# Projection stage of an attention and convolution kernel: row maxima through two pairs of PSUM banks, queries and keys with one bank each

## The chip, the cores and the metric

One NeuronCore of a Trainium2 chip runs the whole program. Its engines are TensorE (PE), VectorE (DVE), ScalarE (ACT), GpSimd (POOL) and SyncE (SP), which issues most of the transfers. They run apart from each other and meet at semaphores. The metric is the device time of one execution in microseconds.

## The reference

The input is x, 2 x 256 x 64 x 64 in f32. Layer 0 is a group norm (32 groups), an attention with 4 heads of 64 channels over the 4096 positions, an output projection and a residual. Layer 1 is batch norm, relu, a 3x3 convolution with one-bit weights, once more the same, and a residual. The part that the change touches, for one batch element:

```python
xn  = group_norm(x, gn_weight, gn_bias)
qkv = einsum('oc,bchw->bohw', qkv_weight, xn) + qkv_bias      # projection
q, k, v = split(qkv, 3, axis=1)                               # 4 heads of 64 channels
attn = softmax(einsum('bhdk,bhdq->bhkq', q, k) / sqrt(64))
out  = einsum('bhkq,bhdq->bhdk', attn, v)
```

## The kernel before, in words

The attention runs over four pairs of heads (two batch elements, two pairs each); a pair fills the 128 partitions. Each pair has a projection stage and then eight query blocks of 512 queries (`query_block`). PSUM has eight banks of 128 x 512 f32. In the query blocks banks 0 to 3 hold the scores (`ps_s`, two slots of two banks), 4 and 5 the products whose maximum is sought (`ps_max`), 6 the output (`ps_o`), and 7 the half sums and the denominators (`ps_misc`).

The projection stage goes over eight blocks `kb` of 512 positions (`kb = n2 * 2 + s`, `s` is 0 or 1). For each block TensorE makes Q (index `j` = 0) and K (`j` = 1), L635, each of two products over the two halves `c` of the channels, and V, L650, of eight small products. These are f32, and each of them stands in the trace as two MATMUL rows, so Q or K is x4 and V is x16. ScalarE copies Q and K to `y32` (L545) and rounds them to f16 as `q_hi` and `k_hi` (L549), and copies V to `vals` (L552). GpSimd makes the rests `q_lo` (L470) and `k_lo` (L477) and normalizes the input two blocks ahead (`xn`, L490), once V of the block that used the same buffer is done. SP loads x for it (L425).

The softmax subtracts a row maximum, which has to be known before the first scores. So the stage also computes maxima. A unit is the product of 128 queries of a block with 512 keys, for two heads: two f16 matmuls (L662) into one pair of banks, and one reduction by VectorE from there (L803). For the first query block there are 32 units: beside block kb (kb = 1 to 7) its four units with the keys of block kb - 1 (`units_beside`), for kb = 4 to 7 one more ("early", it belongs to the second query block), and after block 7 the last four (`last_first_maxima`). `PLACE` numbers the units in the order in which they are issued. The order is written out by hand and is the same on both engines. Below, M0 to M3 are the four units beside a block, E the early one, and L0 to L3 the last four.

All units but L1 and L2 go through `ps_max`. `maxima_of` on TensorE waits until VectorE has reduced all units before (`mx_used`, which starts at 1), and VectorE waits for `mx_ready`. In a block the order is: first product of Q, E, second product of Q, M0, K, M1, half of V, M2, half of V, M3. After L3 VectorE takes the maximum over the blocks (L817), negates it (L820), and TensorE transposes it (`max_rows`, L686) for the scores (L714, L719).

Q and K of block kb go to slot s of `ps_s`, so they have two banks each in turn, and V goes to bank 6 for s = 0 and to bank 7 for s = 1 (`ps_v`). The other users of these banks are waited for: bank 6 is read by the copy of the last pair's output (`o_copied`), bank 7 holds the denominators of the last pair's last query block until VectorE has divided by them (`norm_done`; column sums L694, reciprocal L836, multiplication L845), and `ps_s` holds the output projection at the end of the first batch element (L754), which VectorE reads in `residual` (L899, `x1_ready`).

Of the kernel before, what the change touches and what calls it, by code (L numbers as in the profile page):

```python
# [19 lines left out]
ALU = mybir.AluOpType  # L20
ACT = mybir.ActivationFunctionType
F32 = mybir.dt.float32
F16 = mybir.dt.float16
AX = mybir.AxisListType
RMAX = bass.bass_isa.ReduceOp.max

P = 128
# [339 lines left out]
def attention(nc, x, qkv_t, w0_t, x1_d, g):  # L367
# [4 lines left out]
    with ExitStack() as ctx:  # L372
# [13 lines left out]
        m_part = sb("m_part", [P, 2, 2, UNITS])  # L386
        m_max = sb("m_max", [P, 2 * QT])
        m_neg = sb("m_neg", [P, 2 * QT])
        ps_v = [g.ps_o, g.ps_misc]
        acc_dve = g.ps_misc  # L390

        xn_ready = sem("xn_ready")
# [144 lines left out]
        def _(act):  # L537
            def project(b, hp, n2, s):

                pn = (b * 2 + hp) * NB + n2 * 2 + s  # L540
                for j in range(2):
                    act.wait_ge(g.proj_ready, 4 + pn * 3 + j + 1)

                    act.wait_ge(klo_done if j else qlo_done, 1 + pn)
                    nc.scalar.activation(y32[:, s, j], g.ps_s[:, s, j], ACT.Identity,  # L545
                                         bias=g.qk_bias[:, hp + 2 * j:hp + 2 * j + 1],
                                         scale=g.fscale[:, j:j + 1]).then_inc(y_ready, 1)
                    act.wait_ge(y_ready, 4 + pn * 2 + (j + 1))
                    nc.scalar.activation((k_hi if j else q_hi)[:, cols(n2 * 2 + s)], y32[:, s, j],  # L549
                                         ACT.Copy).then_inc(hi_ready, 1)  # L550
                act.wait_ge(g.proj_ready, 4 + (pn + 1) * 3)
                nc.scalar.activation(vals[:, (n2 * 2 + s) * QT:(n2 * 2 + s + 1) * QT, :],  # L552
                                     ps_v[s].rearrange("p (t d) -> p t d", t=QT), ACT.Copy).then_inc(v_copied, 1)

            def softmax(it, first, last):

# [59 lines left out]
        def _(pe):  # L616
            mm = nc.tensor.matmul

            def project(b, hp, n2, s):

                it0 = (b * 2 + hp) * NB
                pn = it0 + n2 * 2 + s
                pe.wait_ge(g.w_staged, 16 * (b * 2 + hp + 1))
                pe.wait_ge(xn_ready, (pn + 1) * CB)

                pe.wait_ge(y_ready, 2 + pn * 2)
                if n2 == 0:
                    pe.wait_ge(x1_ready, (b * NB + 1 + s) * CB)
                kb = n2 * 2 + s
                these, early = units_beside(kb) if kb else ([], [])  # L630
                if kb > 1:
                    pe.wait_ge(hi_ready, 2 * (it0 + kb - 1))
                for j in range(2):
                    for c in range(CB):
                        ins = mm(g.ps_s[:, s, j], wst[:, c, j, :], xn[:, s, c, :], start=(c == 0), stop=(c == CB - 1))  # L635
                        if c == CB - 1:
                            ins.then_inc(g.proj_ready, 1)
                        if j == 0 and c == 0:
                            maxima_of(it0, early)
                        if kb and c:  # L640
                            if j == 0:
                                pe.wait_ge(hi_ready, 2 * (it0 + kb))
                            maxima_of(it0, these[j:j + 1])
                pe.wait_ge(v_copied, 1 + pn)
                if n2 == 0:

                    pe.wait_ge(norm_done if s else o_copied, it0 * NP + NP if s else it0 + 1)
                for t in range(QT):
                    for c in range(CB):
                        last = mm(ps_v[s][:, t * P:(t + 1) * P], xn[:, s, c, t * P:(t + 1) * P], wst[:, c, 2, :],  # L650
                                  start=(c == 0), stop=(c == CB - 1))
                    if t == 1:
                        maxima_of(it0, these[2:3])
                last.then_inc(g.proj_ready, 1)
                maxima_of(it0, these[3:4])

            def maximum(it0, unit, into):

                block, u = unit
                t, kb = u // NB, u % NB  # L660
                for h in range(2):
                    last = mm(into[:, h], q_hi[own[h], block * TB + t * P:block * TB + (t + 1) * P],  # L662
                              k_hi[own[h], kb * TB:(kb + 1) * TB], start=True, stop=True)
                last.then_inc(mx_ready, 1)

            def maxima_of(it0, units):

                for unit in units:
                    pe.wait_ge(mx_used, 1 + it0 * UNITS + PLACE[unit])
                    maximum(it0, unit, g.ps_max)  # L670

            def last_first_maxima(it0):

                units = units_beside(NB)[0]
                pe.wait_ge(hi_ready, 2 * (it0 + NB))
                pe.wait_ge(mx_used, 1 + it0 * UNITS + PLACE[units[0]])
                maximum(it0, units[0], g.ps_max)
                maximum(it0, units[1], g.ps_s[:, 0])
                maximum(it0, units[2], g.ps_s[:, 1])
                pe.wait_ge(mx_used, 1 + it0 * UNITS + PLACE[units[1]])  # L680
                maximum(it0, units[3], g.ps_max)

            def max_rows(it):
                pe.wait_ge(m_neg_ready, it + 1)
# [102 lines left out]
        def _(dve):  # L787
# [7 lines left out]
            for s in range(2):  # L795
                dve.sem_inc(g.y_out[s], 16)

            def maxima_of(it0, units, where=()):

                for i, unit in enumerate(units):  # L800
                    block, u = unit
                    dve.wait_ge(mx_ready, it0 * UNITS + PLACE[unit] + 1)
                    v.tensor_reduce(m_part[:, block % 2, :, u], where[i] if where else g.ps_max, AX.X,  # L803
                                    ALU.max).then_inc(mx_used, 1)

            def project_step(it0, kb):

                these, early = units_beside(kb)
                maxima_of(it0, early)
                maxima_of(it0, these)  # L810

            def negate_max(it):

# [98 lines left out]
            for b in range(B):  # L912
                for hp in range(2):
                    it0 = (b * 2 + hp) * NB
                    if hp:
                        for part in range(NP):
                            divide(it0 - 1, part)
                    for kb in range(1, NB):
                        project_step(it0, kb)
                    maxima_of(it0, units_beside(NB)[0], (g.ps_max, g.ps_s[:, 0], g.ps_s[:, 1], g.ps_max))  # L920
                    negate_max(it0)
                    write_max_rows(it0, 0)
                    for qb in range(NB):
                        query_block(it0 + qb, qb)
                for n2 in range(NB // 2):
                    if n2 == 1:
                        for part in range(NP):
                            divide((b + 1) * 2 * NB - 1, part)
                    for s in range(2):
                        residual(b, n2, s)  # L930
                        statistics(b, n2, s)
# [370 lines left out]
```

## Time and profile before

| what | us |
|---|---|
| median of 3 runs | 2934.8 (2934.6 to 2935.26) |
| the profiled execution, its time | 2934.27 |
| its span, from the first to the last instruction | 2932.5 |
| mean granted TensorE clock in it | 0.988 |
| TensorE matmul busy | 2793.7 (95%) |
| VectorE busy | 2117.5 (72%) |
| GpSimd busy | 2027.3 (69%) |
| ScalarE busy | 1402.7 (48%) |

Busy is the time in which an engine had an instruction in work; the duration of one is counted from its start to its modelled end. Matmuls overlap: the next starts before the one before has ended, so costs are read from start to start. A bracket behind a row of the timeline gives the idle time of the engine before it and what ended it.

### The profile page before, as it was taken

To read this page: it belongs to the slowest core of one execution; us is meant where nothing else is said; L and a number is where in the kernel's file an instruction comes from. 1 tells how busy PE (TensorE), PEld (TensorE's weight loads), DVE (VectorE), ACT (ScalarE), POOL (GpSimd) and SP (SyncE) were. 2 spreads that over 40 slices of the span, in tenths; PEclk is the share of its full clock that TensorE was granted. 3 is DMA by queue.
4 is the path that set the end of the run, shared out by engine and by line. 5 is a ranking of instruction groups with operands and counts; after the bars stand their busy time and mean duration, and the time that the engine had idled before them with its cause. 6 is when DMAs were issued, how large, how long until landed. Compare 5 with 4: busy or idle time off the path is not lost. (4 is left out here: it accounts for less than half of the span.)

```text
span 2932.5 us, 43630 instructions
## 1 busy us (share of the span) xinstructions
PE 2793.7 (95%) x17060; PEld 1013.2 (35%) x17060; DVE 2117.5 (72%) x2496; ACT 1402.7 (48%) x1477; POOL 2027.3 (69%) x1208
## 2 busy tenths in 40 slices
PE   5899999998999999998999999989999999799898
PEld 3333333333333333343333333343333333244343
DVE  5688888726777888456788888267777885588785
ACT  3355555553555555533555555534555555254342
POOL 2588888893888888844888888947888888500022
PEclk9999999999999999999999999999999999999999
DMA  5000000001000000041000000010000000421022
GB/s 213 35 1 1 1 1 1 1 5 60 1 1 1 1 1 1 1 153 42 1 1 1 1 1 1 1 44 1 1 1 1 1 1 1 148 79 60 15 100 86
DMA packets 26820, 78.27 MB, mean 27 GB/s; under 512 B 1921, under 2 KB 2177, under 8 KB 25601
## 3 DMA queue, kind: packets, MB, share of 16 engines
q1 hardware_dynamic: 25792, 74.19, 7.3%
q8 instruction: 125, 2.05, 0.3%
q10 hardware_dynamic: 832, 1.45, 0.1%
q14 instruction: 71, 0.57, 0.1%
HBM read 58.86 MB, written 16.78 MB: 26 GB/s over the span
## 5 line engine op out<-in xcount | busy, mean ns | idle before, releaser
L512 POOL TENSOR_TENSOR acc_pool<-acc_pool,prob 128x512 f32<-128x512 f32 (+1 forms) x992 | 1781.0, 1795 | 297.5 <-ACT prob L567 177.0
L803 DVE TENSOR_REDUCE m_part<-ps 128x2 f32<-128x1024 f32 x1024 | 1250.6, 1222 | 479.8 <-PE ps L662 456.0
L567 ACT ACTIVATE prob<-ps,exp_scale 128x1024 f32<-128x1024 f32 x1024 | 1086.9, 1111 | 1015.7 <-PE ps L719 1007.8
L703 PE MATMUL ps<-prob,vals 128*64 128x512 f32 x4096 | 990.9, 605 | 0.0
L662 PE MATMUL ps<-k_hi,q_hi 64*128 64x512 f16 x2048 | 394.3, 383 | 45.3 <-DVE m_part L803 45.3
L703 PEld LDWEIGHTS ps<-prob,vals 128*64 128x64 f32 x4096 | 248.7, 136 | 501.9 <-issue 364.2
L714 PE MATMUL ps<-q_hi,k_hi 64*128 64x512 f16 x2048 | 391.1, 379 | 0.0
L714 PE MATMUL ps<-q_hi,k_lo 64*128 64x512 f16 x2048 | 390.4, 378 | 0.0
L719 PE MATMUL ps<-m_rows,shift 64*128 64x512 f16 x2048 | 389.9, 377 | 0.4
L714 PE MATMUL ps<-q_lo,k_hi 64*128 64x512 f16 x2048 | 390.2, 378 | 0.0
L869 DVE TENSOR_TENSOR ps<-ps,prob 128x512 f32<-128x512 f32 x480 | 331.5, 691 | 72.4 <-ACT prob L567 72.4
L662 PEld LDWEIGHTS ps<-k_hi,q_hi 64*128 64x128 f16 x2048 | 99.3, 93 | 529.3 <-DVE m_part L803 405.2
L1135 PE MATMUL ps<-parts,signs 128*128 128x512 f16 x768 | 181.3, 385 | 21.9 <-DVE parts L1194 19.8
L836 DVE RECIPROCAL ps<-ps 128x128 f32<-128x128 f32 x128 | 122.7, 958 | 84.4 <-PE ps L694 84.4
L1135 PE MATMUL ps<-parts,wmid 128*128 128x512 f16 x768 | 178.8, 383 | 0.0
L719 PEld LDWEIGHTS ps<-m_rows,shift 64*128 64x128 f16 x2048 | 99.9, 94 | 125.4 <-DVE m_rows L827 4.0
L714 PEld LDWEIGHTS ps<-q_lo,k_hi 64*128 64x128 f16 x2048 | 100.1, 94 | 122.6 <-issue 2.2
L714 PEld LDWEIGHTS ps<-q_hi,k_hi 64*128 64x128 f16 x2048 | 100.3, 95 | 117.1 <-ACT prob L567 45.4
L714 PEld LDWEIGHTS ps<-q_hi,k_lo 64*128 64x128 f16 x2048 | 100.0, 94 | 113.3 <-issue 1.1
L635 PE MATMUL ps<-xn,wst 128*128 128x512 f32 x256 | 131.3, 628 | 5.0 <-ACT xn L595 4.7
L1085 ACT ACTIVATE parts<-comb 128x512 f16<-128x512 f32 x128 | 77.4, 632 | 105.7 <-DVE comb L1215 105.7
L1135 PEld LDWEIGHTS ps<-parts,signs 128*128 128x128 f16 x768 | 75.2, 98 | 115.9 <-DVE parts L1194 19.9
(109 smaller groups left out, 1408.3 us busy)
## 6 DMA issues: line engine op xcount, KB each, us to landing
xt<-in_x SPq DMA_DIRECT2D x40, 512.0 KB, 4.3
xf<-in_x SPq DMA_DIRECT2D x4, 2048.0 KB, 16.5
x_scratch<-y_tile SPq DMA_DIRECT2D x16, 512.0 KB, 5.0
wf<-in_w_t SPq DMA_DIRECT2D x4, 1152.0 KB, 8.9
rows<-x_scratch SPq DMA_DIRECT2D x8, 576.0 KB, 5.3
rows<-x_scratch SPq DMA_DIRECT2D x8, 544.0 KB, 4.6
xn<-in_x SPq DMA_DIRECT2D x8, 512.0 KB, 5.6
xt<-x_scratch SPq DMA_DIRECT2D x4, 1024.0 KB, 5.1
```

What stands on the lines that cost most here:

```text
L512: nc.gpsimd.tensor_tensor(acc[:, part], acc[:, part], tile[:, part], ALU.add).then_inc(pool_add, 1)
L567: nc.scalar.activation(prob[:, n % PBUF], g.ps_s[:, kt % 2].rearrange("p h n -> p (h n)"), ACT.Exp, scale=g.exp_scale[:]).then_inc(exp_don ...
L635: ins = mm(g.ps_s[:, s, j], wst[:, c, j, :], xn[:, s, c, :], start=(c == 0), stop=(c == CB - 1))
L662: last = mm(into[:, h], q_hi[own[h], block * TB + t * P:block * TB + (t + 1) * P], k_hi[own[h], kb * TB:(kb + 1) * TB], start=True, stop=True)
L703: last = mm(g.ps_o[own[h], :], vals[:, kt, own[h]], prob[:, n % PBUF, h * TB:(h + 1) * TB], start=(kt == 0), stop=(kt == KT - 1))
L714: mm(g.ps_s[:, kt % 2, h], k[own[h], keys], q[own[h], cols(qb)], start=(k is k_hi and q is q_hi), stop=False)
L719: last = mm(g.ps_s[:, kt % 2, h], shift[own[h]], m_rows[own[h], qb % 2], start=False, stop=True)
L803: v.tensor_reduce(m_part[:, block % 2, :, u], where[i] if where else g.ps_max, AX.X, ALU.max).then_inc(mx_used, 1)
L836: v.reciprocal(g.ps_misc[:, c], g.ps_misc[:, c]).then_inc(rec_ready, 1)
L869: v.tensor_tensor(acc_dve, acc_dve, tile, ALU.add).then_inc(dve_add, 1)
L1085: nc.scalar.activation(parts[:, k % 2, c, 0, pos, :, 1:W + 1], comb[:, c, pos], ACT.Copy).then_inc(hi_done, 1)
L1135: last = nc.tensor.matmul(g.ps[:, 4 * m + pos, :], weights(l, c, pos, dx)[:, m * P:(m + 1) * P], parts[:, s, c, h, pos, :, dx:dx + W], sta ...
```

## The change

The pairs of banks in the projection stage are laid out anew. The maxima go in turn through banks 4, 5 and banks 6, 7 (`max_pair`, by the parity of `PLACE`), and TensorE waits only until the unit before the last one is reduced. Q has bank 0 and K bank 1 for every block, V has bank 2 for s = 0 and bank 3 for s = 1. The units are issued in twos: Q, E if there is one, K, M0 and M1, all of V, M2 and M3. The waits for other users of the banks move with them: `o_copied` and `norm_done` before the first unit of block 1, `x1_ready` for the second slot of the output projection before V of block 0. Q and K each wait until ScalarE has read that of the block before (`y_ready`). The last four units: L0 and L1 through the two pairs, L2 through banks 0 and 1, L3 through the pair of L1. VectorE's order of units is as before, and nothing is added to or taken from the work.

```diff
--- before.py
+++ after.py
@@ -386,7 +386,7 @@
         m_part = sb("m_part", [P, 2, 2, UNITS])
         m_max = sb("m_max", [P, 2 * QT])
         m_neg = sb("m_neg", [P, 2 * QT])
-        ps_v = [g.ps_o, g.ps_misc]
+        max_pair = [g.ps_max, g.ps[:, 6:8, :]]
         acc_dve = g.ps_misc
 
         xn_ready = sem("xn_ready")
@@ -542,7 +542,7 @@
                     act.wait_ge(g.proj_ready, 4 + pn * 3 + j + 1)
 
                     act.wait_ge(klo_done if j else qlo_done, 1 + pn)
-                    nc.scalar.activation(y32[:, s, j], g.ps_s[:, s, j], ACT.Identity,
+                    nc.scalar.activation(y32[:, s, j], g.ps[:, j], ACT.Identity,
                                          bias=g.qk_bias[:, hp + 2 * j:hp + 2 * j + 1],
                                          scale=g.fscale[:, j:j + 1]).then_inc(y_ready, 1)
                     act.wait_ge(y_ready, 4 + pn * 2 + (j + 1))
@@ -550,7 +550,8 @@
                                          ACT.Copy).then_inc(hi_ready, 1)
                 act.wait_ge(g.proj_ready, 4 + (pn + 1) * 3)
                 nc.scalar.activation(vals[:, (n2 * 2 + s) * QT:(n2 * 2 + s + 1) * QT, :],
-                                     ps_v[s].rearrange("p (t d) -> p t d", t=QT), ACT.Copy).then_inc(v_copied, 1)
+                                     g.ps[:, 2 + s].rearrange("p (t d) -> p t d", t=QT),
+                                     ACT.Copy).then_inc(v_copied, 1)
 
             def softmax(it, first, last):
 
@@ -623,36 +624,39 @@
                 pe.wait_ge(g.w_staged, 16 * (b * 2 + hp + 1))
                 pe.wait_ge(xn_ready, (pn + 1) * CB)
 
-                pe.wait_ge(y_ready, 2 + pn * 2)
-                if n2 == 0:
-                    pe.wait_ge(x1_ready, (b * NB + 1 + s) * CB)
                 kb = n2 * 2 + s
                 these, early = units_beside(kb) if kb else ([], [])
-                if kb > 1:
-                    pe.wait_ge(hi_ready, 2 * (it0 + kb - 1))
+                if kb == 0:
+                    pe.wait_ge(x1_ready, (b * NB + 1) * CB)
                 for j in range(2):
+                    pe.wait_ge(y_ready, 3 + pn * 2 + j)
                     for c in range(CB):
-                        ins = mm(g.ps_s[:, s, j], wst[:, c, j, :], xn[:, s, c, :], start=(c == 0), stop=(c == CB - 1))
-                        if c == CB - 1:
-                            ins.then_inc(g.proj_ready, 1)
-                        if j == 0 and c == 0:
-                            maxima_of(it0, early)
-                        if kb and c:
-                            if j == 0:
-                                pe.wait_ge(hi_ready, 2 * (it0 + kb))
-                            maxima_of(it0, these[j:j + 1])
+                        ins = mm(g.ps[:, j], wst[:, c, j, :], xn[:, s, c, :], start=(c == 0), stop=(c == CB - 1))
+                    ins.then_inc(g.proj_ready, 1)
+                    if j == 0:
+                        first_maxima(it0, early)
+                if kb:
+                    pe.wait_ge(hi_ready, 2 * (it0 + kb))
+                    if kb == 1:
+                        pe.wait_ge(o_copied, it0 + 1)
+                        pe.wait_ge(norm_done, it0 * NP + NP)
+                    first_maxima(it0, these[0:2])
                 pe.wait_ge(v_copied, 1 + pn)
-                if n2 == 0:
-
-                    pe.wait_ge(norm_done if s else o_copied, it0 * NP + NP if s else it0 + 1)
+                if kb == 0:
+                    pe.wait_ge(x1_ready, (b * NB + 2) * CB)
                 for t in range(QT):
                     for c in range(CB):
-                        last = mm(ps_v[s][:, t * P:(t + 1) * P], xn[:, s, c, t * P:(t + 1) * P], wst[:, c, 2, :],
+                        last = mm(g.ps[:, 2 + s, t * P:(t + 1) * P], xn[:, s, c, t * P:(t + 1) * P], wst[:, c, 2, :],
                                   start=(c == 0), stop=(c == CB - 1))
-                    if t == 1:
-                        maxima_of(it0, these[2:3])
                 last.then_inc(g.proj_ready, 1)
-                maxima_of(it0, these[3:4])
+                first_maxima(it0, these[2:4])
+
+            def first_maxima(it0, units):
+
+                for unit in units:
+                    i = PLACE[unit]
+                    pe.wait_ge(mx_used, it0 * UNITS + max(i, 1))
+                    maximum(it0, unit, max_pair[i % 2])
 
             def maximum(it0, unit, into):
 
@@ -673,12 +677,9 @@
 
                 units = units_beside(NB)[0]
                 pe.wait_ge(hi_ready, 2 * (it0 + NB))
-                pe.wait_ge(mx_used, 1 + it0 * UNITS + PLACE[units[0]])
-                maximum(it0, units[0], g.ps_max)
-                maximum(it0, units[1], g.ps_s[:, 0])
-                maximum(it0, units[2], g.ps_s[:, 1])
-                pe.wait_ge(mx_used, 1 + it0 * UNITS + PLACE[units[1]])
-                maximum(it0, units[3], g.ps_max)
+                first_maxima(it0, units[0:2])
+                maximum(it0, units[2], g.ps_s[:, 0])
+                first_maxima(it0, units[3:4])
 
             def max_rows(it):
                 pe.wait_ge(m_neg_ready, it + 1)
@@ -795,19 +796,28 @@
             for s in range(2):
                 dve.sem_inc(g.y_out[s], 16)
 
-            def maxima_of(it0, units, where=()):
-
+            def maximum(it0, unit, source):
+
+                block, u = unit
+                dve.wait_ge(mx_ready, it0 * UNITS + PLACE[unit] + 1)
+                v.tensor_reduce(m_part[:, block % 2, :, u], source, AX.X, ALU.max).then_inc(mx_used, 1)
+
+            def maxima_of(it0, units):
+
+                for unit in units:
+                    maximum(it0, unit, g.ps_max)
+
+            def first_maxima(it0, kb):
+
+                these, early = units_beside(kb)
+                for unit in early + these:
+                    maximum(it0, unit, max_pair[PLACE[unit] % 2])
+
+            def last_first_maxima(it0):
+
+                units = units_beside(NB)[0]
                 for i, unit in enumerate(units):
-                    block, u = unit
-                    dve.wait_ge(mx_ready, it0 * UNITS + PLACE[unit] + 1)
-                    v.tensor_reduce(m_part[:, block % 2, :, u], where[i] if where else g.ps_max, AX.X,
-                                    ALU.max).then_inc(mx_used, 1)
-
-            def project_step(it0, kb):
-
-                these, early = units_beside(kb)
-                maxima_of(it0, early)
-                maxima_of(it0, these)
+                    maximum(it0, unit, g.ps_s[:, 0] if i == 2 else max_pair[PLACE[unit] % 2])
 
             def negate_max(it):
 
@@ -916,8 +926,8 @@
                         for part in range(NP):
                             divide(it0 - 1, part)
                     for kb in range(1, NB):
-                        project_step(it0, kb)
-                    maxima_of(it0, units_beside(NB)[0], (g.ps_max, g.ps_s[:, 0], g.ps_s[:, 1], g.ps_max))
+                        first_maxima(it0, kb)
+                    last_first_maxima(it0)
                     negate_max(it0)
                     write_max_rows(it0, 0)
                     for qb in range(NB):
```

## Rows read from the trace of the kernel before

**Rows 1.** The page, part 1: busy time of each engine and its share.

```profile
PE 2793.7 (95%) x17060; PEld 1013.2 (35%) x17060; DVE 2117.5 (72%) x2496; ACT 1402.7 (48%) x1477; POOL 2027.3 (69%) x1208
```

**Rows 2.** Windows (PE PEld DVE ACT POOL busy; PEclk; DMA): stage, block, tail, clock.

```profile
37.90:113.00 75.10, 63.39 (x268) 30.45 (x268) 44.25 (x38) 28.62 (x42) 27.61 (x28) 0.97 0.22 75
...
77.39:86.58 9.19, 8.09 (x37) 3.71 (x35) 6.13 (x5) 3.41 (x6) 3.83 (x5) 1.00 0.01 3
...
110.00:112.00 2.00, 0.00 (x0) 0.00 (x0) 1.89 (x4) 0.00 (x0) 0.00 (x0) 0.50 1.04 394
...
662.00:663.00 1.00, 1.00 (x7) 1.00 (x6) 0.92 (x1) 0.00 (x0) 0.00 (x0) 0.50 0.08 16
```

**Rows 3.** Timeline, TensorE, first pair: V of block 0, then block 1.

```profile
42.81 1.95 PE L650 MATMUL ps<-wst,xn 128*128 128x128 f32 x16
44.60 1.88 PE L635 MATMUL ps<-xn,wst 128*128 128x512 f32 x4
46.41 0.39 PE L662 MATMUL ps<-k_hi,q_hi 64*128 64x512 f16 x2
46.73 1.98 PE L635 MATMUL ps<-xn,wst 128*128 128x512 f32 x4
48.65 0.39 PE L662 MATMUL ps<-k_hi,q_hi 64*128 64x512 f16 x2
...
50.36 0.39 PE L662 MATMUL ps<-k_hi,q_hi 64*128 64x512 f16 x2 [0.24 <-DVE m_part L803]
...
52.40 1.98 PE L635 MATMUL ps<-xn,wst 128*128 128x512 f32 x4
```

**Rows 4.** Timeline, TensorE, first pair: parts of block 5, starts of 6 and 7.

```profile
77.39 1.12 PE L635 MATMUL ps<-xn,wst 128*128 128x512 f32 x2
78.78 0.39 PE L662 MATMUL ps<-k_hi,q_hi 64*128 64x512 f16 x2 [0.27 <-DVE m_part L803]
...
80.59 0.39 PE L662 MATMUL ps<-k_hi,q_hi 64*128 64x512 f16 x2 [0.36 <-DVE m_part L803]
...
86.58 1.13 PE L635 MATMUL ps<-xn,wst 128*128 128x512 f32 x2
...
95.77 1.12 PE L635 MATMUL ps<-xn,wst 128*128 128x512 f32 x2
```

**Rows 5.** Timeline, first pair: M3 of block 7, last four units, max_rows.

```profile
104.64 0.39 PE L662 MATMUL ps<-k_hi,q_hi 64*128 64x512 f16 x2 [0.24 <-DVE m_part L803]
...
106.44 0.82 PE L662 MATMUL ps<-k_hi,q_hi 64*128 64x512 f16 x6 [1.42 <-DVE m_part L803]
106.87 4.62 DVE L803 TENSOR_REDUCE m_part<-ps 128x2 f32<-128x1024 f32 x4 [0.57 <-PE ps L662]
...
112.10 1.01 PE L686 MATMUL ps<-const,m_neg 128*4 128x128 f32 x4 [3.55 <-DVE m_neg L820]
```

**Rows 6.** Timeline, second pair, block 1: the divisions, M1 and its wait.

```profile
655.38 1.98 PE L635 MATMUL ps<-xn,wst 128*128 128x512 f32 x4
...
660.17 0.29 DVE L845 TENSOR_TENSOR o_all<-o_raw,ps 128x128 f32<-128x128 f32 x1
...
661.64 0.39 PE L662 MATMUL ps<-k_hi,q_hi 64*128 64x512 f16 x2 [2.04 <-DVE m_part L803]
...
661.96 2.08 PE L650 MATMUL ps<-wst,xn 128*128 128x128 f32 x8
...
666.31 1.99 PE L635 MATMUL ps<-xn,wst 128*128 128x512 f32 x4
```

**Rows 7.** Timeline, third pair: last residual, loads, block 1, xn of block 2.

```profile
1295.69 1.41 DVE L899 SCALAR_TENSOR_TENSOR y_tile<-ps,proj_bias,xt 128x512 f32<-128x512 f32 x2 [0.53 <-DMA x_scratch<-y_tile]
...
1297.86 13.12 SPq L425 DMA_DIRECT2D xt<-in_x  x4
...
1299.17 1.88 PE L635 MATMUL ps<-xn,wst 128*128 128x512 f32 x4
...
1304.41 1.52 POOL L490 TENSOR_SCALAR xn<-xt,gn_a,gn_b 128x512 f32<-128x512 f32 x2 [5.74 <-DMA xt<-in_x]
```

## The prediction

> **What bounds the kernel now.** I began with the page's busy times: TensorE is busy 95% of the span, the others 72% or less [rows 1], so the question is what TensorE waits for. Then I laid windows over the four projection stages, which the change alone touches. The first lasts 75.1 us, and in it TensorE has matmuls in work for 63.4 us; inside it a block of 9.19 us has 8.09 us of them, VectorE 6.13, ScalarE 3.41 and GpSimd 3.83 [rows 2]. So in a block no engine but TensorE is near full, and TensorE is not full either. The timeline of the stage shows why: before a unit TensorE stands idle for 0.24 to 0.36 us, released by VectorE's reduction [rows 3, 4].
>
> The loop behind it can be measured. Two units that wait for each other stand 1.71 us apart (48.65 to 50.36) [rows 3]: 0.43 us from the first matmul to the reduction's start (104.64 to 105.07), 1.23 for the reduction [rows 5], and the rest, 0.05, to the next matmul. Between two units TensorE has 1.47 us of other work in the V part (1.71 less the 0.24 idle) and 1.44 between E and its neighbours (1.81 less 0.36), so it waits; only over a whole K has it 2.24, so it doesn't [rows 3]. That is two waits in a block of four units, four in a block of five.
>
> There is a second cost, which isn't idle time. A unit alone takes 0.32 us (46.41 to 46.73) [rows 3]. Three without anything between take 0.82 until the last has ended, and one 0.39 [rows 5]: each further one costs (0.82 - 0.39) / 2 = 0.215. Also the f32 products around a unit are dearer: two rows after a unit take 1.12 and four 1.98 [rows 3, 4], so a row costs 0.43 in the run, but four of them until the next unit can start take 1.92 (46.73 to 48.65), or 1.81 where no unit stood ahead (44.60 to 46.41). Breaking the f32 stream for a unit costs some 0.3 us on top of the unit's 0.215.
>
> The Trainium skill ("TensorEngine Tiling (Array Packing)", Key Properties) says that a change of the tiling mode drains TensorE; units use 64-row tiles and the projections whole ones, and the trace's 0.3 us agrees.
>
> **The change part by part.** *A block of four units.* Q and K follow each other: 1.81 + 4 x 0.43 = 3.53. M0 and M1: 0.215 + 0.32 = 0.54. V in one piece: half of it takes 1.71 - 0.32 - 0.24 = 1.15 until the unit behind it [rows 3], and the other eight rows 1.79 / 16 = 0.112 each (42.81 to 44.60) [rows 3], so 2.05. M2 and M3: 0.54. Sum 6.66. Does VectorE keep up? M1's reduction starts behind M0's. Four queued reductions take 4.62 us [rows 5], that is (4.62 - 1.23) / 3 = 1.13 from start to start, so M1's is done 0.43 + 1.13 + 1.23 = 2.79 after M0's start, and M3, which takes its banks, may start at 2.84. TensorE gets there at 0.54 + 2.05 + 0.215 = 2.80: a wait of 0.04. So block 1 takes 6.7 in place of 7.80 (44.60 to 52.40) [rows 3], 1.1 less; blocks 2 and 3 have the same parts: 3 x 1.1 = 3.3.
>
> *A block of five.* 1.92 (Q) + 0.32 (E) + 1.92 (K) + 0.54 + 2.05 + 0.54 + 0.04 = 7.3 in place of 9.19 (77.39 to 86.58, 86.58 to 95.77) [rows 4]: 1.9 less, for blocks 4 to 6: 5.7. VectorE needs 5 x 1.13 = 5.7 us of that, E's banks are free (M2 is reduced 2 us before), and M1 finds E's reduction done.
>
> *Block 7 and the end.* Here VectorE becomes the bound, since eight reductions stand behind K. M0 starts 4.16 us after the block (1.92 + 0.32 + 1.92), its reduction at 4.59; M2 comes at 4.16 + 0.54 + 2.05 = 6.75 and its reduction can start at 7.18 where VectorE was ready at 6.85: 0.33 lost. Eight reductions take 7 x 1.13 + 1.23 = 9.14. The last ends at 14.06. From there to max_rows it takes what it takes now, 112.10 - (106.87 + 4.62) = 0.61 [rows 5]. So 14.7 in place of 112.10 - 95.77 = 16.33 [rows 4, 5]: 1.7 less. About 1.1 of the TensorE gain of this block is given back here.
>
> Per pair 3.3 + 5.7 + 1.7 = 10.7, four pairs 42.8.
>
> *The moved waits.* In the second and fourth pair, VectorE divides for the last pair before any unit. Now M0 goes ahead and M1 waits 2.04 us for divisions plus M0's reduction; then the granted clock is 0.50, the 1.2 GHz level, and half of V takes 2.08; block 1 lasts 655.38 to 666.31, 10.93 [rows 2, 6]. In the new order M0 waits for norm_done (660.17 + 0.29 = 660.46) [rows 6], an idle of 1.5 behind Q and K, but M1 waits no more. From 660.5 on: 0.54 + 2.05 + 0.54 + 0.04 gives the next Q at 663.7, 2.6 less than now and 1.5 beyond the 1.1 counted above. If the clock falls again as it does now, behind the shorter idle, up to 1.4 of that is lost (4.67 us from M1 to Q now, against 3 x 0.32 + 2 x 1.15 = 3.26). I take 0.8 for each of the two pairs: 1.6. Queued behind the waiting M0 on TensorE are V of block 1 and all that follows; VectorE waits for M0 alone.
>
> V of block 0 in the third pair now waits for the last residual, done at 1295.69 + 1.41 = 1297.10; K ends at 1297.3, so nothing. But xn of block 2 is ready only at 1304.41 + 1.52 = 1305.93, held by the load issued at 1297.86, and block 2's Q will be wanted at 1299.17 + 6.7 = 1305.9 [rows 7]: just hidden, uncovered by each further gain.
>
> *Costed at nothing:* the single banks of Q and K. ScalarE reads Q while TensorE does K, V and the units, with 3.41 us of work in a block [rows 2]; K's bank is wanted again a block later. V keeps two banks. GpSimd's 3.83 in 7.3 leaves its rests and xn time.
>
> Sum: 42.8 + 1.6 = 44.4. The profiled execution took 2934.27 (span 2932.5, 1.8 around it), 0.5 under the median, so it would take 2889.9, and the median 2890.4.
>
> **Bounds.** Reductions in twos may start 1.28 apart (1.23 + 0.05) instead of 1.13: 0.15 for each of 7 M3s and 7 intervals at the end, 2.1 a pair. The low clock at the end of the stage, 0.50 before max_rows [rows 2], may begin earlier or later: up to 1.4 either way, by the same loss as in block 1. M0 is issued 0.1 later than the loop of 1.71 explains in block 5 (1.81) [rows 4], it has two waits; in all blocks that is 0.7 a pair. The two places above: 1.6 and 1 once. Least gain 44.4 - 4 x (2.1 + 1.4 + 0.7) - 2.6 = 25, most 44.4 + 4 x 1.4 + 1.4 = 51.
>
> **Rivals.** (1) *The two pairs don't overlap*: VectorE's reduction of one pair hinders TensorE's next unit and units stay 1.71 apart. A block of four takes 4 x 1.71 = 6.84, one of five 8.55, block 7 to max_rows 4.59 + 7 x 1.71 + 1.23 + 0.61 = 18.4, so 1.0 x 3 + 0.6 x 3 - 2.1 = 2.7 a pair, 11 in all: 2924. Against it: VectorE takes units from three pairs at 1.13 while TensorE has written them [rows 5]. 5%.
>
> (2) *The gain is swallowed by the input*: xn of block k + 2 becomes the bound. The loop is load, 6.5 us in the third pair (1297.86 to 1304.41), and 1.52 of GpSimd, 8.1 for two blocks that take 13.4 [rows 7]. It would need loads of 17 us to keep today's pace in the blocks of five. Result within 3 us of 2934.8. 3%.
>
> (3) *Slower: the clock falls in the stage.* It falls behind idles such as the 2.04 us [rows 2, 6], and the new order ends the units of a block in bursts. At 0.50 the work of a block, 6.7 to 7.3, takes about double, some 6 more; the gain of a pair, 10.7, is gone once two of its seven blocks run so. All seven: 4 x (7 x 6 - 10.7) = 125 slower. For it: one fall in the second pair; against it: idle in a block drops from 1.1 to 0.04, and block 5 has no fall now [rows 2]. 3%; I put its time at 2950. The Trainium skill ("TensorE: Matmul & The Clock Gate", A second HAM failure mode: psum-queue depth-cycling) warns that short idles between groups of matmuls, as TensorE cycles through banks, can make its clock swing; by it this rival would hold, and the block at PEclk 1.00 with four such idles [rows 2] speaks against it here.
>
> **How the numbers follow.** The forecast's mechanism has 89%, and its bounds 2884 to 2910; the ends of them need all terms to go one way. I take 2883 to 2905, which leaves out its last tail (5%) and the rivals (11%). A measurement of this kernel tells 0.2% (6 us) from no change. Faster: 89 + 5 = 94%; same: 3%; slower: 3%.
>
> **What would show it.** In the profile after: L662 in x4 rows of the timeline, blocks of 6.7 and 7.3 us; hardly any TensorE idle by L803 in blocks; VectorE the bound from block 7's K to max_rows with 14.7; in the second pair one idle of 1.5 ahead of M0. All of it the same in four pairs, and the query blocks unchanged. It is wrong if units in a two are more than 0.25 apart, if PEclk is below 1.00 inside blocks 2 to 6, or if TensorE waits there for xn or y.

## The result and the profile after

| | before | after |
|---|---|---|
| median of the runs, us | 2934.89 (5 runs, 2934.6 to 2935.26) | 2890.99 (5 runs, 2888.16 to 2894.52) |
| ratio, 95% interval | | 0.9849 (0.9839 to 0.9860) |
| the profiled execution: time, span, us | 2934.27, 2932.5 | 2894.52, 2892.7 |
| mean granted TensorE clock in it | 0.988 | 0.986 |

The change makes the kernel 43.9 us faster; 44.4 were forecast. The profiled execution of after is the slowest of its five, 3.5 us above the median, and its span is only 39.8 us shorter. Where these microseconds are is part of the question below.

The page of the kernel after: busy times, and the group of all units of the kernel. The last columns are TensorE's idle time ahead of them, 26.5 us in all.

```profile
PE 2777.9 (96%) x17060; PEld 1010.5 (35%) x17060; DVE 2112.2 (73%) x2496; ACT 1402.0 (48%) x1477; POOL 2026.8 (70%) x1208
...
L666 PE MATMUL ps<-k_hi,q_hi 64*128 64x512 f16 x2048 | 388.7, 383 | 26.5 <-DVE m_part L803 23.2
```

TensorE's timeline in the first pair, blocks 1, 4 and the start of 5, which answer to [rows 3, 4]:

```profile
44.99 3.60 PE L634 MATMUL ps<-xn,wst 128*128 128x512 f32 x8
48.52 0.60 PE L666 MATMUL ps<-k_hi,q_hi 64*128 64x512 f16 x4
49.06 2.05 PE L649 MATMUL ps<-wst,xn 128*128 128x128 f32 x16
51.04 0.72 PE L666 MATMUL ps<-k_hi,q_hi 64*128 64x512 f16 x4
51.69 3.70 PE L634 MATMUL ps<-xn,wst 128*128 128x512 f32 x8
...
65.29 1.98 PE L634 MATMUL ps<-xn,wst 128*128 128x512 f32 x4
67.21 0.39 PE L666 MATMUL ps<-k_hi,q_hi 64*128 64x512 f16 x2
...
69.44 0.61 PE L666 MATMUL ps<-k_hi,q_hi 64*128 64x512 f16 x4
...
72.61 1.98 PE L634 MATMUL ps<-xn,wst 128*128 128x512 f32 x4
```

The units stand as x4 rows, two at a time, and no row of a block has a bracket. One short wait is left inside the second two: M3 starts 0.72 - 0.39 = 0.33 us after M2, where M1 starts 0.60 - 0.39 = 0.21 after M0 (0.39 is one unit alone). M3 takes the banks of M1, whose reduction ends at 48.96 + 2.36 = 51.32, and M3 starts at 51.04 + 0.33 = 51.37:

```profile
48.96 2.36 DVE L803 TENSOR_REDUCE m_part<-ps 128x2 f32<-128x1024 f32 x2 [13.23 <-PE ps L666]
```

The granted clock over blocks 4 to 6 (the figure behind the five busy times) is 1.00:

```profile
65.29:87.25 21.96, 21.96 (x104) 10.85 (x102) 17.82 (x16) 10.23 (x16) 12.34 (x13) 1.00 0.08 25
```

Block 1 takes 51.69 - 44.99 = 6.70 us, where it took 7.80, and block 4 takes 72.61 - 65.29 = 7.32, where it took 9.19. The whole of V between two units is 51.04 - 49.06 = 1.98. The wait of M3 is some 0.11, where 0.04 was forecast, and V is 0.07 shorter than the 2.05 of the sum, so the block comes out the same.

The end of the stage, which answers to [rows 5]:

```profile
87.25 1.98 PE L634 MATMUL ps<-xn,wst 128*128 128x512 f32 x4
...
95.73 0.39 PE L666 MATMUL ps<-k_hi,q_hi 64*128 64x512 f16 x2 [1.09 <-DVE m_part L803]
96.78 0.61 PE L666 MATMUL ps<-k_hi,q_hi 64*128 64x512 f16 x4 [0.65 <-DVE m_part L803]
99.04 0.39 PE L666 MATMUL ps<-k_hi,q_hi 64*128 64x512 f16 x2 [1.66 <-DVE m_part L803]
101.85 1.01 PE L687 MATMUL ps<-const,m_neg 128*4 128x128 f32 x4 [2.42 <-DVE m_neg L830]
```

From Q of block 7 to max_rows it takes 101.85 - 87.25 = 14.60 us, where it took 16.33. Here the brackets are back: L0, L1, L3 and max_rows all wait for VectorE.

The starts of Q of block 0 and of max_rows give the four stages, and the rest lies between them:

| us | before | after | less |
|---|---|---|---|
| stage of pair 1 | 74.18 | 63.95 | 10.23 |
| stage of pair 2 | 77.92 | 65.90 | 12.02 |
| stage of pair 3 | 72.80 | 63.84 | 8.96 |
| stage of pair 4 | 77.95 | 65.91 | 12.04 |
| all the rest of the span | 2629.65 | 2633.10 | -3.45 |

So the stages give 43.25 us, and 3.45 are lost outside them in this execution.

### The profile page after: what moved, and what is told of

It is laid out like the page before. It is cut to its first block and busy times, and to the rows that moved or that the text cites. A ratio compares the mean times of both kernels' runs of the same rounds, so it can differ in the third digit from the quotient of the medians.

```text
span 2892.7 us, 43602 instructions
## 1 busy us (share of the span) xinstructions
PE 2777.9 (96%) x17060; PEld 1010.5 (35%) x17060; DVE 2112.2 (73%) x2496; ACT 1402.0 (48%) x1477; POOL 2026.8 (70%) x1208
## 3 DMA queue, kind: packets, MB, share of 16 engines
q8 instruction: 125, 2.05, 0.3%
## 5 line engine op out<-in xcount | busy, mean ns | idle before, releaser
L666 PE MATMUL ps<-k_hi,q_hi 64*128 64x512 f16 x2048 | 388.7, 383 | 26.5 <-DVE m_part L803 23.2
L634 PE MATMUL ps<-xn,wst 128*128 128x512 f32 x256 | 124.1, 618 | 5.3 <-ACT xn L596 4.7
```

The source lines that it names most:

```text
L634: ins = mm(g.ps[:, j], wst[:, c, j, :], xn[:, s, c, :], start=(c == 0), stop=(c == CB - 1))
```

## The experiments

All are variants of the changed kernel. Each is compared by its ratio to the kernel before, timed beside it on the same chip; medians of before there were 2933.07 (E1 to E4), 2935.68 (E5, E6 and E8) and 2935.37 (E9, E10).

| | median us | ratio to before, 95% interval |
|---|---|---|
| the change | 2890.99 | 0.9849 (0.9839 to 0.9860) |
| E1 layout only | 2934.34 | 1.0005 (0.9996 to 1.0015) |
| E2 ones, two pairs | 2899.10 | 0.9883 (0.9867 to 0.9900) |
| E3 twos, one pair | 2973.30 | 1.0136 (1.0120 to 1.0153) |
| E4 the change again | 2888.94 | 0.9849 (0.9833 to 0.9866) |
| E5 block 7 reordered | 2882.48 | 0.9824 (0.9810 to 0.9837) |
| E6 fill | 2884.40 | 0.9825 (0.9811 to 0.9838) |
| E7 V of block 0 in bank 6 | 2892.25 | one run |
| E8 E5 and E6 | 2879.13 | 0.9806 (0.9793 to 0.9820) |
| E9 E7 again | 2889.31 | 0.9843 (0.9828 to 0.9859) |
| E10 E8 and E7 | 2879.24 | 0.9809 (0.9796 to 0.9822) |

**E1, the layout alone.** Q, K and V lie as in the change; the units have the order of before and one pair of banks. The last four units go as before too, but for L2, which takes banks 6 and 7. Those lines and VectorE's side are not shown here.

```diff
 for c in range(CB):
     ins = mm(g.ps[:, j], wst[:, c, j, :], xn[:, s, c, :], ...)
+    if j == 0 and c == 0:
+        first_maxima(it0, early)
+    if kb and c:
...
+        first_maxima(it0, these[j:j + 1])
...
+    if t == 1:
+        first_maxima(it0, these[2:3])
 last.then_inc(g.proj_ready, 1)
-first_maxima(it0, these[2:4])
+first_maxima(it0, these[3:4])
...
-    pe.wait_ge(mx_used, it0 * UNITS + max(i, 1))
-    maximum(it0, unit, max_pair[i % 2])
+    pe.wait_ge(mx_used, it0 * UNITS + i + 1)
+    maximum(it0, unit, g.ps_max)
```

> Q and K with one bank each and V with banks 2 and 3 as in the changed kernel, but the units in the order of before, one at a time through one pair of banks. Theory (the gain comes from the second pair of banks and from the twos, and the single banks of Q and K cost nothing): blocks of 7.9 and 9.2 us as before, about 2935 us, at most 1 more for the later V of block 0 in the third pair. Rival (the moved waits and the layout give part of the gain themselves): under 2928 us.

Measured: ratio 1.0005, no difference. TensorE's timeline, a block of five:

```profile
69.69 1.12 PE L634 MATMUL ps<-xn,wst 128*128 128x512 f32 x2
71.09 0.39 PE L670 MATMUL ps<-k_hi,q_hi 64*128 64x512 f16 x2 [0.27 <-DVE m_part L809]
...
72.89 0.39 PE L670 MATMUL ps<-k_hi,q_hi 64*128 64x512 f16 x2 [0.36 <-DVE m_part L809]
...
78.88 1.13 PE L634 MATMUL ps<-xn,wst 128*128 128x512 f32 x2
```

9.19 us for the block and waits of 0.27 and 0.36 as in [rows 4]. The single banks of Q and K cost nothing and the layout gives nothing; the rival fell.

**E2, two pairs of banks, but one unit at a time.** The edit of E1 without its last two lines (and with the last four units as in the change): the order of before, in the banks of the change.

> The changed kernel, but each unit stands alone where it stood before (Q in two parts, V in two halves, a unit behind each); both pairs of banks in use. Theory (0.3 us for each break of the f32 stream beside the waits): no wait for VectorE is left, blocks of four take 7.3 and blocks of five 7.85 us, block 7 to max_rows 14.4; 7.2 us a pair better than before, about 2904 us. Rival (the breaks cost nothing, all of the gain is waits): the blocks take 6.8 and 7.3 us and the time is 2891.

Measured: ratio 0.9883, 34 us less than before (0.0117 x 2935), 10 more than the change. Its timeline, block 2, and the starts of 4 and 5:

```profile
53.02 1.98 PE L634 MATMUL ps<-xn,wst 128*128 128x512 f32 x4
...
60.32 1.98 PE L634 MATMUL ps<-xn,wst 128*128 128x512 f32 x4
...
67.61 1.13 PE L634 MATMUL ps<-xn,wst 128*128 128x512 f32 x2
...
75.42 1.12 PE L634 MATMUL ps<-xn,wst 128*128 128x512 f32 x2
```

No unit waits, and yet block 2 takes 7.30 (53.02 to 60.32) and block 4 takes 7.81 (67.61 to 75.42), against 6.8 and 7.32 in the change. These 0.5 us a block are the two breaks that the change takes out. The rival, by which breaks cost nothing, fell. A block of five goes from 9.19 to 7.81 by the second pair of banks and to 7.32 by the twos: 1.38 and 0.49, where the prediction had 1.1 of waits and 0.6 for two breaks. The time was 5 us better than forecast: some 4 of that are the second and fourth pair, whose block 1 the sum had left out (their stages took 67.9, 10.0 less than before; from block 1 on the first pair gained 8.0).

The Trainium skill ("TensorEngine Tiling (Array Packing)", Key Properties) says that a change of tiling mode drains TensorE. E2 against the change agrees with it, 0.5 us for two breaks, but doesn't tell the drain from anything else that a break costs.

**E3, twos through one pair of banks.** The last two lines of the edit of E1 alone, with the last four units as in E1.

> The order of the changed kernel, in twos, but all units of blocks 1 to 7 through banks 4 and 5, so that the second of a two waits for the first's reduction. Theory: each of the 14 seconds a pair waits 1.5 us (0.43 + 1.23 + 0.05 less the first's 0.215); blocks take 9.7 and 10.2 us, 10 us a pair worse than before, about 2975 us. Rival (fewer breaks carry the gain, the waits hide): 2918 us.

Measured: ratio 1.0136, 40 us slower than before. The timeline shows M2 and M3 of block 2, then the starts of blocks 3 and 4:

```profile
62.39 0.39 PE L666 MATMUL ps<-k_hi,q_hi 64*128 64x512 f16 x2
64.11 0.39 PE L666 MATMUL ps<-k_hi,q_hi 64*128 64x512 f16 x2 [1.33 <-DVE m_part L805]
64.43 3.70 PE L634 MATMUL ps<-xn,wst 128*128 128x512 f32 x8
...
74.12 1.98 PE L634 MATMUL ps<-xn,wst 128*128 128x512 f32 x4
```

The second of a two starts 1.72 us after the first, 1.33 of it idle, and a block of four takes 9.69 (64.43 to 74.12), as forecast. So the order in twos without the second pair of banks is a loss; the two parts of the change don't add, the second needs the first.

**E4, the changed kernel again.**

> The changed kernel once more, unchanged. Its times lay between 2888.2 and 2894.5 us where those of before lay within 0.7 us. Theory (the low clock around max_rows lasts a different time in each pair and each execution: in the profile shown it lasted some 2 us longer in the second and fourth pair): the stages up to max_rows repeat within 0.5 us, the time differs by a few us, and the difference lies in the first query block of a pair. Rival (the input loads differ between executions): the difference lies in the stages, as idle of TensorE ahead of a block's Q.

Measured: 2887.3 to 2891.5 us, median 2888.94, span of the profile 2888.5, 4.2 less than in the first profile. The stages took 65.16, 65.92, 63.42 and 65.88. Pairs 2 and 4 repeat within 0.03; pair 1 took 1.2 more (Q and K of its first block took 6.52 us, 44.73 - 38.21, where the first profile has 43.21 - 37.90 = 5.31), pair 3 took 0.4 less. From max_rows of pair 2 to the output projection it took 1242.08 - 705.99 = 536.09, against 1242.45 - 704.17 = 538.28 in the first profile (and 1262.26 - 726.02 = 536.24 before). Windows of the change's first profile there, the clock being the figure behind the five busy times:

```profile
700.00:702.00 2.00, 0.61 (x2) 0.11 (x2) 2.00 (x3) 0.00 (x0) 0.00 (x0) 0.58 0.94 285
712.00:714.00 2.00, 2.00 (x12) 0.76 (x10) 0.61 (x1) 0.91 (x1) 0.56 (x1) 0.51 0.00 0
```

and of E4:

```profile
702.00:704.00 2.00, 0.61 (x2) 0.10 (x2) 2.00 (x2) 0.00 (x0) 0.00 (x0) 0.76 0.90 250
...
710.00:712.00 2.00, 0.67 (x8) 0.16 (x6) 1.23 (x1) 1.36 (x2) 1.40 (x2) 1.00 0.00 0
```

In the first profile the clock is at 0.58 in the window from 700 and still at 0.51 in the one from 712; in E4 it is at 0.76 from 702 and back at 1.00 from 710. The kernel before, for comparison:

```profile
722.00:724.00 2.00, 0.39 (x2) 0.10 (x2) 2.00 (x3) 0.00 (x0) 0.00 (x0) 0.85 0.97 263
730.00:732.00 2.00, 0.80 (x6) 0.11 (x2) 1.15 (x1) 1.40 (x2) 1.21 (x2) 0.95 0.00 0
```

Behind pair 4 it is the same. From its max_rows to the convolutions the first profile has 2529.28 - 1939.84 = 589.44, E4 2524.99 - 1938.98 = 586.01 and before 2569.20 - 1981.31 = 587.89. In the first profile of the change the clock is still low in a window 8 to 10 us after max_rows (first line); in the kernel before it is almost back in one 5 to 7 us after its own (second line):

```profile
1948.00:1950.00 2.00, 2.00 (x14) 0.71 (x10) 0.28 (x1) 1.11 (x1) 0.28 (x2) 0.60 0.03 8
...
1986.00:1988.00 2.00, 0.68 (x6) 0.11 (x4) 1.23 (x1) 1.11 (x1) 1.31 (x2) 0.92 0.00 0
```

The theory held for where most of the difference lies. It missed in the stages: pair 1 did not repeat within 0.5 us. And the scatter isn't new: in the later runs before itself scattered from 2930.8 to 2937.0.

**E5, block 7 reordered.**

```diff
-    return own, [(1, kb - (NB - 2 * LEAD))] if kb >= NB - 2 * LEAD else []
+    return own, [(1, kb - (NB - 1 - 2 * LEAD))] if NB - 1 - 2 * LEAD <= kb < NB - 1 else []
...
 if j == 0:
     first_maxima(it0, early)
+    if kb == NB - 1:
+        pe.wait_ge(hi_ready, 2 * (it0 + kb))
+        first_maxima(it0, these[0:2])
+        these = these[2:]
```

> The changed kernel, with the four early units beside blocks 3 to 6 in place of 4 to 7, and in block 7 M0 and M1 between Q and K, M2 and M3 behind K. Theory (from K of block 7 on VectorE's queue of eight reductions is the bound): block 3 grows to 7.3, the time from block 7 to max_rows shrinks from 14.6 to 12.8; 1.3 us a pair better, about 2884 beside 2889 to 2891 of the changed kernel. Rival (the end is held by something else, the copies of K and V or k_lo): block 7 to max_rows stays above 14, and the time is 2 us worse for the longer block 3.

Measured: ratio 0.9824, 7.3 us better than the change (0.0025 x 2935), where 5 were expected. Its timeline from Q of block 7:

```profile
88.40 1.98 PE L634 MATMUL ps<-xn,wst 128*128 128x512 f32 x4
...
95.47 0.82 PE L670 MATMUL ps<-k_hi,q_hi 64*128 64x512 f16 x6
98.31 0.39 PE L670 MATMUL ps<-k_hi,q_hi 64*128 64x512 f16 x2 [2.02 <-DVE m_part L807]
101.12 1.01 PE L691 MATMUL ps<-const,m_neg 128*4 128x128 f32 x4 [2.42 <-DVE m_neg L834]
```

Block 7 to max_rows takes 101.12 - 88.40 = 12.72. L0 to L2 go out behind V without a wait, since VectorE has been served earlier. VectorE's queue was the bound at the end, as the prediction had it. The stages of pairs 2 and 4 are 1.4 us shorter, 5.5 for four pairs. The third stage took 60.79 in this profile, 3.05 less than in the first profile of the change and 2.63 less than in E4: neither V of block 0 nor Q of block 2 waited there. So 1.2 to 1.7 us beyond the edit's own 1.4 come from a residual and a load that were done early (the load 5.9 us after its issue), which differs between executions of one kernel. That would be most of the rest of the 7.3; for the executions without a profile it isn't shown. The mean granted clock of this profile is 0.990 where the change had 0.986 and 0.987.

**E6, fill.**

```diff
+FILL = (2, 2, 6, 9)
...
+def fill(n):
+
+    for _ in range(n):
+        for h in range(2):
+            mm(g.ps[:, 2 + h], q_hi[own[h], 0:P], k_hi[own[h], 0:TB], start=True, stop=True)
...
-first_maxima(it0, units[0:2])
+pe.wait_ge(v_copied, 2 + it0 + NB)
+fill(FILL[0])
+first_maxima(it0, units[0:1])
+fill(FILL[1])
+first_maxima(it0, units[1:2])
 maximum(it0, units[2], g.ps_s[:, 0])
+fill(FILL[2])
 first_maxima(it0, units[3:4])
+fill(FILL[3])
```

> The changed kernel plus 19 products a pair that nobody reads, in twos of 64-row matmuls into banks 2 and 3, while TensorE waits at the end of the stage (2 before L0, 2 before L1, 6 before L3, 9 before max_rows). Theory (the idle there makes the clock fall, and the low level lasts into the first query block): the granted clock stays at 1.00, max_rows comes no later, and 1.5 to 4 us a pair are saved in max_rows and the first scores: 2881, and the executions lie closer together. Rival (the clock falls all the same, or the low clock lies under the wait for VectorE): no change, or 1 us a pair worse.

Measured: ratio 0.9825, 7.0 us better than the change (0.0024 x 2935), less than the forecast 10. TensorE's timeline from Q of block 7:

```profile
88.42 1.98 PE L635 MATMUL ps<-xn,wst 128*128 128x512 f32 x4
...
103.01 0.60 PE L700 MATMUL ps<-const,m_neg 128*4 128x128 f32 x4 [0.48 <-DVE m_neg L843]
...
105.10 0.39 PE L733 MATMUL ps<-m_rows,shift 64*128 64x512 f16 x2 [0.73 <-DVE m_rows L850]
```

and its windows over the end of the stage (PEclk is the figure behind the five busy times):

```profile
99.00:101.00 2.00, 1.64 (x16) 0.60 (x14) 2.00 (x3) 0.00 (x0) 0.00 (x0) 1.00 1.01 372
103.00:105.00 2.00, 1.35 (x10) 0.48 (x10) 1.32 (x2) 0.00 (x0) 0.00 (x0) 1.00 0.11 37
```

The clock stays at 1.00 to the end, and max_rows comes as late as in the change (14.59 after Q of block 7). max_rows and the scores then run at full rate, but the first that needs the maxima now waits 0.73 us for VectorE's m_rows, so part of the gain is given back. The executions lie within 3.4 us where the change's lay within 6.4, and within 4.2 in E4.

**E7, V of block 0 in bank 6**, which doesn't wait for the residual.

```diff
 if kb == 1:
-    pe.wait_ge(o_copied, it0 + 1)
+    pe.wait_ge(v_copied, 2 + pn)
     pe.wait_ge(norm_done, it0 * NP + NP)
...
 if kb == 0:
+    pe.wait_ge(o_copied, it0 + 1)
+if kb == 1:
     pe.wait_ge(x1_ready, (b * NB + 2) * CB)
...
-last = mm(g.ps[:, 2 + s, ...
+last = mm(g.ps[:, 2 + s if kb else 6, ...
```

> The changed kernel with V of block 0 in bank 6, so that it doesn't wait for the last residual of the first batch element; block 1 waits for it before its V. Theory (in the third pair the input of block 2 is the bound behind it): the 0.84 us ahead of V of block 0 go, the 0.65 ahead of Q of block 2 grow to 1.5, the stage stays at 63.8. Rival (the two add up): the third stage takes 63.0.

Measured: the third stage took 62.06, less than the theory's 63.8 and the rival's 63.0. V of block 0 started without a wait, and so did Q of block 2: the load of x, issued at 1278.04, 4.2 us after Q of block 0, had landed by 1283.63, 5.6 us later. The change's first profile had 1278.75, 5.05 after Q of block 0, and 1285.79, 7.0 later.

**E9, the same again,** to see which of these stays.

> The kernel of e7_v0_bank6 once more. There the wait ahead of Q of block 2 didn't appear, since the load of x landed 5.6 us after its issue and not 7.0 as in the changed kernel. Theory (the landing decides, and it differs between executions): V of block 0 starts without a wait again; Q of block 2 waits as far as the load's landing, counted from its issue, lies beyond 6.2 us; the whole is at most 1.5 us better than the changed kernel. Rival (the bank alone decides): no wait ahead of Q of block 2 whatever the landing.

Measured: ratio 0.9843, not apart from the change. Timeline of the third pair, whose Q of block 0 starts at 1273.89:

```profile
1277.40 1.95 PE L651 MATMUL ps<-wst,xn 128*128 128x128 f32 x16
...
1278.91 9.94 SPq L425 DMA_DIRECT2D xt<-in_x  x3
...
1286.69 1.52 POOL L490 TENSOR_SCALAR xn<-xt,gn_a,gn_b 128x512 f32<-128x512 f32 x2 [8.02 <-DMA xt<-in_x]
...
1288.32 4.24 PE L634 MATMUL ps<-xn,wst 128*128 128x512 f32 x6 [2.37 <-issue]
```

This time the load took 1286.69 - 1278.91 = 7.8 us, and TensorE stood idle 2.37 ahead of Q of block 2; the stage took 65.97. The theory's 6.2 accounts for 1.6 of the 2.37. The other 0.8 is the issue, 5.02 us after Q of block 0 where E7 had 4.17. So the time at which the input is there decides, which is the residual's end and the landing together, and moving V only moves the idle time. The rival fell.

**E8 and E10, together.** E8 is the edit of E5 and, before L3 and before max_rows, 7 and 9 unread twos. E10 adds E7.

> The edits of e5_front7 and e6_fill together (7 unread twos before L3, 9 before max_rows). Theory: both gains add, 1.3 and 1.5 to 4 us a pair: 2874 to 2880. Rival (the fill delays L3 or max_rows, or the clock falls all the same): 2884 or more.

> The edits of e8_front7_fill and e7_v0_bank6 together. Theory: 0.8 to 1.5 us better than e8_front7_fill in the third pair alone, 2878. Rival: the same within the scatter, 2879 to 2880.

Measured: 0.9806 and 0.9809. E8 is 12.6 us better than the change (0.0043 x 2935), 1.7 short of the sum of E5 and E6, and 57 better than before. E10 gives no more: in its profile Q of block 2 in the third pair waited 2.54 us for an input that landed 8.4 us after its issue (the stage took 65.00, against 61.21 in E8), so its own theory, 0.8 to 1.5 better, didn't hold.

## Why the prediction was right, point by point

*The blocks.* Forecast 6.7 and 7.3, measured 6.70 (6.80 where a unit stands ahead) and 7.32; blocks 3 to 6 take the same in all four pairs. Both parts of the cost are shown: the waits by E1 against E2, the breaks by E2 against the change. Of 44 us, 34 come with the second pair of banks while units stand alone, 10 from the twos. The rival by which the pairs don't overlap is out: M1 follows M0 by 0.21 us. But one of the prediction's own signs of being wrong came up, units of a two more than 0.25 apart: M2 and M3 are 0.33 apart in every block. The sum had M3's wait, at 0.04 where it is 0.11, and the sign was drawn tighter than the sum's error allowed. It cost nothing here, since V was as much shorter.

*Block 7 and the end.* Forecast 14.7, measured 14.60. That VectorE's eight reductions are the bound was shown by E5, which serves it earlier and takes 1.9 us off (0.5 of them come back in block 3, to which the early unit moves).

*Block 1 of the second and fourth pair.* M0 waited 1.62 us (forecast 1.5):

```profile
645.52 3.70 PE L634 MATMUL ps<-xn,wst 128*128 128x512 f32 x8
...
650.30 0.29 DVE L855 TENSOR_TENSOR o_all<-o_raw,ps 128x128 f32<-128x128 f32 x1
...
650.85 0.61 PE L666 MATMUL ps<-k_hi,q_hi 64*128 64x512 f16 x4 [1.62 <-ACT k_hi L549]
```

The bracket names k_hi, but M0 doesn't wait for k_hi of its own block in the code: `hi_ready` is asked for block 0's there. What it waits for is `norm_done`, and the last division ends at 650.30 + 0.29 = 650.59, 0.26 before M0 starts. The block, with the granted clock as the figure behind the five busy times:

```profile
645.52:654.02 8.50, 6.88 (x35) 3.64 (x33) 7.32 (x11) 3.35 (x5) 4.17 (x6) 1.00 0.20 65
```

It took 8.50, 0.2 more than worked out for a full clock, which is that 0.26, and V behind the idle ran at its full rate. The clock did not fall as it does behind the 2.04 of [rows 6], so the loss of 0.7 a pair that I had put into the sum stayed away. The two pairs gave 12.03 where 10.7 + 0.8 was forecast: the term was 0.5 a pair too small.

*The third pair.* This is the step that failed, though the total came out: "K ends at 1297.3, so nothing". The rows of the change:

```profile
1276.58 1.41 DVE L909 SCALAR_TENSOR_TENSOR y_tile<-ps,proj_bias,xt 128x512 f32<-128x512 f32 x2 [1.82 <-DMA x_scratch<-y_tile]
...
1278.14 2.02 PE L649 MATMUL ps<-wst,xn 128*128 128x128 f32 x16 [0.84 <-DVE y_tile L909]
...
1278.75 13.61 SPq L425 DMA_DIRECT2D xt<-in_x  x4
...
1285.79 1.52 POOL L490 TENSOR_SCALAR xn<-xt,gn_a,gn_b 128x512 f32<-128x512 f32 x2 [7.39 <-DMA xt<-in_x]
...
1287.41 3.67 PE L634 MATMUL ps<-xn,wst 128*128 128x512 f32 x8 [0.65 <-issue]
```

The last residual ended at 1277.99, 4.3 us after Q of block 0 (3.2 in [rows 7]), because VectorE had waited for the store that frees its tile; TensorE stood idle 0.84 ahead of V. Then the load, issued only behind the residual, landed later, and TensorE stood idle 0.65 ahead of Q of block 2 (the bracket says "issue", but the xn that Q needs was done at 1285.79 + 1.52 = 1287.31, 0.1 before). That is the prediction's third sign of being wrong, TensorE waiting for xn, in this one block. The step took the store's and the load's times from one execution as fixed. The stage gave 8.96 in place of 10.7, and 1.49 of the 1.74 are these two idles. E7, E9 and E10 show landings of 5.6, 7.8 and 8.4 us for the same load, and the idle time behind following them.

*The other rivals.* The input became a bound in the third pair alone, at a cost of 0.65 us, and the clock is 1.00 in the blocks (65.29 to 87.25 and 645.52 to 654.02, above): neither took the gain.

*The low clock at the end.* I had left it at nothing, with 1.4 a pair either way. It is the size of the scatter: 3.45 us are lost outside the stages in the first profile, and what follows pairs 2 and 4 is 2.04 us (538.28 against 536.24) and 1.55 us (589.44 against 587.89) longer than before, 3.6 in all. Behind both the windows under E4 show the low clock lasting longer than before, and in E4, where it didn't, these two stretches are no longer than before. That the idle at the end of the stage causes it is shown by E6: filled, the clock stays at 1.00, and 7 us are gained.

*The sum.* Stages 43.25 against 44.4, the errors being +1.0 (pairs 2 and 4), -1.7 (pair 3) and -0.5 (pair 1). Of the last, 0.4 is the first block, 7.09 us in place of 6.68. Its Q and K take 5.31 us in the changed kernel, where those of block 1 take 48.52 - 44.99 = 3.53, though the granted clock is 1.00 in a window over it; what slows it is open. The median came out 0.6 us from the forecast; that it is so near is luck of these errors and of the low clock.

## What to carry to other kernels

When an engine waits for a buffer between its own pieces of work, count the loop (write, reduce, release) against the work that lies between two uses: a second buffer is worth the difference, once for each place where it is positive, and no more. Two uses of two buffers may then be put side by side, which saves the switch between kinds of matmul, but only then: with one buffer the same order lost 40 us (E3). And at the end of a stage look for the queue that is left on the other engine: serving it earlier and keeping TensorE from idling there gave another 12.6 us.

## What the runs showed that I had not expected

An idle of 1.62 us ahead of M0 left the clock alone and one of 2.04 ahead of M1 did not, in the same block of the second pair. At the end of the stage, once the clock had fallen, it stayed low for about 13 us in one execution of the changed kernel and 7 in another (second pair, by windows of 2 us). Unread matmuls in the idle time, 19 twos a pair, were worth 7 us. And one load of x of 512 KB landed 5.6 to 8.4 us after its issue in the same place of the program, right behind a store.
